# The next sequence's attention entry moved beside the experts, on one PSUM bank

## The reference, cut to what matters

```python
x = x + L0_attn(_layernorm(x))   # one head, softmax over queries, only the diagonal is used
x = x + L0_ffn(_layernorm(x))    # 2 layers: token shift, 8 heads of 64 with local windows of 64,
                                 # l2-normed rotary q and k, then norm, w1, gelu gate (341), w2
x = x + L1_attn(_layernorm(x))   # causal attention, 16 heads of 8, then Wo
x = x + L1_ffn(_layernorm(x))    # softmax router, top 2 of 8 experts, plus a shared expert:
    # y += gate[e] * (silu(x @ w_gate[e]) * (x @ w_up[e])) @ w_down[e]
```

## Time and profile before

| | us |
|---|---|
| median of three runs | 1863.35 (1860.35 to 1864.81) |
| profiled execution, its own time | 1865.29 |
| its span, first to last instruction | 1863.5 |
| busy PE / DVE / ACT / POOL | 1598.5 / 1239.7 / 926.7 / 594.0 |
| mean granted TensorE clock | 0.937 of full speed |

### The profile page before, as it was taken

How to read it: one execution, slowest core, us unless ns; L and a number is a source line. 1 busy time by engine, 2 the same in 40 slices (tenths; PEclk the granted TensorE clock), 3 DMA queues, 4 the chain that set the end, 5 groups by cost and what they waited for, 6 DMA issues and landing times.

```text
span 1863.5 us, 29596 instructions
## 1 busy us (share of the span) xinstructions
PE 1598.5 (86%) x11565; PEld 934.8 (50%) x11632; DVE 1239.7 (67%) x2636; ACT 926.7 (50%) x1751; POOL 594.0 (32%) x401
## 2 busy tenths in 40 slices
PE   5688876799979899799988999798996889788978
PEld 2354443446454555546555455545553546445635
DVE  6866767775677657595577756786576447674724
ACT  3465653466543844457544664438443444352241
POOL 2756726151160604324061511606043014110000
PEclk9789998799989999899998999899997899898989
DMA  4200100300131011500123001310114002304102
GB/s 120 66 1 21 27 1 20 69 23 17 41 89 32 22 32 34 111 23 2 41 68 69 22 24 34 92 29 22 32 40 105 3 18 76 78 11 103 37 1 63
DMA packets 37291, 80.12 MB, mean 43 GB/s; under 512 B 6782, under 2 KB 22654, under 8 KB 33776
## 3 DMA queue, kind: packets, MB, share of 16 engines
q1 hardware_dynamic: 37152, 78.22, 16.7%
HBM read 54.74 MB, written 8.78 MB: 34 GB/s over the span
## 4 chain that ended last, share of the span: by engine, by line
PE 47%; DVE 23%; ACT 14%; POOL 12%; issue 4%; DMA 0%; SPq 0%; POOLq 0%; DVEq 0%; ACTq 0%
PE ps L455 42%; POOL fsmall L1348 5%; DVE bsmall L1224 5%; ACT bigs L944 5%; PE ps L460 4%; POOL work L1371 3%; ACT work L870 3%; DVE fsmall L1113 2%; POOL work L1382 2%; POOL bsmall L1348 1%; DVE fsmall L1105 1%; DVE bxn L1021 1%; DVE work L1076 1%; DVE work L1075 1%; DVE fxn L1021 1%
## 5 line engine op out<-in xcount | busy, mean ns | idle before, releaser
L1348 POOL TENSOR_TENSOR fsmall<-fsmall,consts 128x8 f32<-128x8 f32 (+1 forms) x140 | 200.1, 1440 | 330.5 <-DVE fsmall L1015 310.9
L455 PE MATMUL ps<-maskb,identb 128*128 128x128 bf16 (+1 forms) x1122 | 227.8, 239 | 31.3 <-ACT work L870 18.8
L455 PE MATMUL ps<-bxt,mw 128*128 128x512 f32 x504 | 246.7, 610 | 5.9 <-DVE bigs L1320 5.9
L1371 POOL TENSOR_TENSOR work<-work 128x1024 f32<-128x1024 f32 x56 | 132.2, 2360 | 351.0 <-DVE work L1076 351.0
L870 ACT ACTIVATE work<-ps,fsmall 128x128 f32<-128x128 f32 x448 | 164.0, 493 | 71.1 <-DVE fsmall L1117 70.4
L460 PE MATMUL ps<-ident,work 128*128 128x128 f32 x924 | 140.6, 298 | 50.2 <-ACT work L870 42.4
L1224 DVE TENSOR_REDUCE bsmall<-ps 128x1 f32<-128x512 f32 (+3 forms) x308 | 175.3, 631 | 7.5 <-PE ps L455 6.8
L455 PE MATMUL ps<-wqkv,h 128*128 128x512 f32 x336 | 163.4, 618 | 14.1 <-ACT vs L830 8.8
L1402 POOL TENSOR_TENSOR work<-work,fsmall 128x1024 f32<-128x1024 f32 x56 | 106.2, 1897 | 216.1 <-DVE fsmall L1108 216.1
L944 ACT ACTIVATE bigs<-ps 128x512 f32<-128x512 f32 x280 | 146.1, 635 | 24.1 <-PE ps L455 23.7
L966 ACT ACTIVATE bigs<-ps 128x512 f32<-128x512 f32 x126 | 75.3, 598 | 156.6 <-PE ps L455 155.9
(11 more groups left out here) (327 smaller groups left out, 2962.7 us busy)
## 6 DMA issues: line engine op xcount, KB each, us to landing
mw<-in_experts SPq DMA_DIRECT2D x63, 384.0 KB, 3.1
pks<-scr_partsb SPq DMA_DIRECT2D x42, 192.0 KB
pqs<-scr_partsb SPq DMA_DIRECT2D x126, 64.0 KB
v2s<-vs SPq DMA_DIRECT2D x14, 512.0 KB, 4.7
v2s<-vs SPq DMA_DIRECT2D x14, 384.0 KB, 6.3
scr_partsb<-bigs SPq DMA_DIRECT2D x7, 768.0 KB, 3.7
wqkv<-in_experts SPq DMA_DIRECT2D x9, 384.0 KB, 3.1
xin<-in_x SPq DMA_DIRECT2D x7, 256.0 KB, 3.5
```

Of the source, the lines that this page charges most:

```text
L455: return nc.tensor.matmul(o, a, b, start=start, stop=stop, skip_group_check=True)
L1348: return nc.gpsimd.tensor_tensor(out, x, consts[:, k:k + 1].broadcast_to([x.shape[0], x.shape[1]]), op)
L1371: nc.gpsimd.tensor_tensor(R.qk[:, m, :], R.qk[:, m, :], R.part[m % 2], ALU.add).then_inc(R.l_add.sem, 1)
```

## The change

Lane B's entry for back s+1 is a generator of its own, `enter`, and is drawn beside the experts of back s: `beside` lets an entry stage go once the expert named in `ENTRY_AFTER` has passed. Back 0's entry stands behind `front0`; back 7's entry stays where it was. The entry uses bank 2 alone for the transposes, q, k and v, one after the other, so k waits for q's copy, v for k's copy. While it does, gate and up share two banks (`expert_banks`): a gate waits for the silu of the half expert before, an up for the multiply of the half expert before. In backs 6 and 7 there are three banks as before; back 0's and back 7's entries still use four. The normalised x goes to `bxe` in `ctmp`, the silu results have three buffers instead of four, so that `big[0]` to `big[2]` are free for the parts.

```diff
+ENTRY_AFTER = {"ln": 0, "xn": 1, "tp": 2, "q": 3, "k": 4, "v": 5, "parts": 5, "parts1": 5, "parts2": 6, "parts3": 6, "va": 5,
+               "save": 7}
+ENTRY_BANKS = [2, 2, 2, 2]
+def beside(experts, entry):
+    waiting = next(entry, None)
+    for name in experts:
+        e = int(name[3]) if name.startswith("moe") else int(name[2]) + 1
+        while waiting and e > ENTRY_AFTER[waiting]:
+            yield "n." + waiting
+            waiting = next(entry, None)
+        yield name
+    while waiting:
+        yield "n." + waiting
+        waiting = next(entry, None)
...
-        self.qkf, self.qkr, self.oc = ctmp[:, 0:2, :], ctmp[:, 2:4, :], ctmp
+        self.qkf, self.qkr, self.bxe, self.oc = ctmp[:, 0:2, :], ctmp[:, 2:4, :], ctmp[:, 2, :], ctmp
-        self.silu = [[self.big[2 * i + c] for c in range(2)] for i in range(2)]
+        self.silu = [self.big[i] for i in (3, 8, 9)]
...
+        def follows(R, s):
+            return R is backs and s + 1 < R.count
+        def expert_banks(R, s):
+            return 2 if follows(R, s) else 3
+        def entry_banks(R, s):
+            return [R.bb[i] for i in (ENTRY_BANKS if R is backs and s else range(4))]
...
+            def enter(R, s):
+                bt, bq, bk, bv = entry_banks(R, s)
                 yield "tp"
                 pe.wait_ge(R.b_xn.sem, R.b_xn.at(s, 1))
-                turn_tiles(R.bb[0], lambda tt: R.bxn[:, tt, :]).then_inc(R.b_tp.sem, 1)
-                yield "qkv"
+                turn_tiles(bt, lambda tt: R.bxn[:, tt, :]).then_inc(R.b_tp.sem, 1)
+                yield "q"
                 pe.wait_ge(R.b_xt.sem, R.b_xt.at(s, 1))
-                mm(R.bb[1], cw[:, 0, :], R.bxt[:, :]).then_inc(R.c_qkv.sem, 1)
-                mm(R.bb[2], cw[:, 1, :], R.bxt[:, :]).then_inc(R.c_qkv.sem, 1)
+                mm(bq, cw[:, 0, :], R.bxe).then_inc(R.c_qkv.sem, 1)
+                yield "k"
+                if bk is bq:
+                    pe.wait_ge(R.c_qkf.sem, R.c_qkf.at(s, 1))
+                mm(bk, cw[:, 1, :], R.bxe).then_inc(R.c_qkv.sem, 1)
+                yield "v"
+                if bv is bk:
+                    pe.wait_ge(R.c_qkf.sem, R.c_qkf.at(s, 2))
                 for tt in range(NT):
-                    i = mm(R.bb[3][:, tt * P:(tt + 1) * P], R.bxt[:, tt * P:(tt + 1) * P], cw[:, 2, :])
+                    i = mm(bv[:, tt * P:(tt + 1) * P], R.bxe[:, tt * P:(tt + 1) * P], cw[:, 2, :])
                 i.then_inc(R.c_qkv.sem, 1)
...
+                yield from beside(experts(R, s), enter(R, s + 1) if follows(R, s) else iter(()))
+            def experts(R, s):
+                banks = expert_banks(R, s)
...
-                            if n >= 3:
-                                q = n - 3
+                            if n >= banks:
+                                q = n - banks
                                 freed = R.m_hid if q % 2 else R.m_silu
                                 pe.wait_ge(freed.sem, freed.at(s, q // 2 + 1))
-                            mm(R.bb[n % 3], R.mw[:, e % SLOTS, j * MH + c * P:j * MH + (c + 1) * P], R.bxt[:, :]).then_inc(done.sem, 1)
+                            mm(R.bb[n % banks], R.mw[:, e % SLOTS, j * MH + c * P:j * MH + (c + 1) * P], R.bxt[:, :]).then_inc(done.sem, 1)
...
```

More of the change, by code:

```diff
@@ L56 @@
     "tensor": (
[L57 to L66, removed]
@@ L123, with ahead @@
 EXP_AT = exp_places()
+ENTRY_AFTER = {"ln": 0, "xn": 1, "tp": 2, "q": 3, "k": 4, "v": 5, "parts": 5, "parts1": 5, "parts2": 6, "parts3": 6, "va": 5,
+               "save": 7}
+ENTRY_BANKS = [2, 2, 2, 2]
+def ahead(entry):
+    return ("n." + name for name in entry)
+def beside(experts, entry):
[9 more added lines that the diff above has]
+        waiting = next(entry, None)
 def run_lanes(engine, order, front_lane, back_lane):
@@ L1174, in front, with enter @@
                 finish(R.fv)
-            def back(R, s):
+                if R is front0:
+                    yield from ahead(enter(backs, 0))
+            def enter(R, s):
                 R.bv.start()
@@ L1199, in back @@
                 tt_(R.parts[:, :, 2, :], R.qkr, R.parts[:, :, 1, :], ALU.subtract).then_inc(R.c_parts.sem, 1)
-                yield "va"
-                dve.wait_ge(R.c_qkv.sem, R.c_qkv.at(s, 3))
-                cp(R.va[:, :, :, 0:CD], R.bb[3][:, :].rearrange("p (a b c) -> p a b c", a=NT, c=CD)).then_inc(R.c_v.sem, 1)
+            def back(R, s):
+                x2q = x2[:, (R.first + s) % 3, :, :]
+                if R is back7:
+                    yield from enter(R, s)
                 def split_maxima(r, bank):
@@ L1297, in back, with experts @@
                 dve.wait_ge(R.r_w.sem, R.r_w.at(s, 1))
+                finish(R.bv)
+                yield from beside(experts(R, s), enter(R, s + 1) if follows(R, s) else iter(()))
+            def experts(R, s):
+                banks = expert_banks(R, s)
                 def add_expert(e):
@@ L1426, in back @@
                 finish(R.bp)
+                if follows(R, s):
+                    yield from ahead(enter(R, s + 1))
             run_lanes(pool, ORDER["gpsimd"], *both_lanes(front, back, fronts, front0, backs, back7))
@@ L1473, in front, with enter @@
                     yield from project(R, s, l)
-            def back(R, s):
-                last = s == R.count - 1
-                yield "parts"
+                if R is front0:
+                    yield from ahead(enter(backs, 0))
+            def enter(R, s):
+                yield "save"
                 sp.wait_ge(R.c_parts.sem, R.c_parts.at(s, 1))
@@ L1499, in back, with experts @@
                     sp.dma_start(R.pq[r][96:99, :, :], R.scrm.rearrange("k (a c) b -> k a (c b)", a=RH)).then_inc(R.c_mpacked.sem, 16)
+                yield from beside(experts(R, s), enter(R, s + 1) if follows(R, s) else iter(()))
+            def experts(R, s):
+                last = s == R.count - 1
                 for e in range(1, ALL):
```

93 lines of the change are left out of this document (58 added, 35 removed).

## The result

| kernel | median, us | runs | ratio to before |
|---|---|---|---|
| before | 1864.08 | 1860.35 to 1865.37 | |
| changed | 1835.59 | 1834.02 to 1835.88 | 0.9858 (0.9837 to 0.9879) |

The changed kernel is faster by 28.5 us, 1.4% (1.2 to 1.6%). The profiled execution took 1835.7 us with a span of 1833.9, against 1863.5 before.

A forecast was written before the change was run, and what follows sets the result against it. No engine reaches 90% (PE 86%); the chain of waits bounds the kernel, with the entry on it in the opening. Openings -32, first opening 0, experts' stretches +32.5, last part -30: -29.5, median 1834 us, range 1810 to 1860.

The forecast's parts named there:

- The opening: Front's local attention without the entry beside it: 8 us less per turn (5 to 9), -32 over four turns.
- The experts' stretch: Experts with the next entry beside them: 6.5 us more per turn, +32.5 over five turns (+5 to +60).
- The last part: After the turns, where backs set the pace: -19.5, +5 and -19.5 sum to -34, taken as -30 (-12 to -36).
- The signs: Profile: POOL roots 452 us over two turns; wrong if PE's waits for the multiply grow to tens of us.
- Rival 3: Last part gives only 12, as the seventh front or back 6's packed data come after the back: 1852, chance 0.14.
- Rival 5: Experts' stretch: two of four parts operations wait for a POOL sum of 2.36 us, +23.5: 1857, chance 0.05.
- the rule weighed in the prediction: A two-port DVE conversion or two-SBUF-input operation and a POOL instruction lock each other out for a whole instruction.
- two banks, 1.0 us: Early experts' stretch: an up waits for the previous half expert's multiply, 3 us late, two hidden: 1.0 per turn.
- rival 4: Two banks make PE wait for DVE, from moe61u to moe71u: 7.5 us more per turn, 1871, chance 0.14.
- The split of the +6.5: Experts' stretch: q and k 1.8, order 1.95, parts 0.3 and 1.9, moe61u -0.7, banks 1.0; sum 6.3, taken as 6.5.
- The first turn's opening: Back 0's entry pieces lie on DVE ahead of the front; it ends at 352 against 351.7: 0 (-5 to +5).
- rival 2: Experts' stretch hides nearly all of the entry, costing 2.5 us per turn: -51.5, 1812, chance 0.20.

The follow-up runs named there:

- e2: Changed kernel with back 0's entry put back in its old place in the first turn, all others ahead: 1832.45 us, ratio 0.9819 to the kernel before.
- e1: Kernel before with gate and up of backs 0 to 5 on two banks instead of three, entries and order as before: 1938.73 us, ratio 1.0411.
- e6: Kernel before with the changed kernel's order in the five turns, entries in old places, gate and up there on two banks: 1883.83 us, ratio 1.0110.
- e11: e1 with VectorE's dn1 and moe30u put ahead of the front's w1a0.1, w1a1.1, w1a2.1 in the five turns: 1921.60 us, ratio 1.0308.
- e8: Changed kernel with four front stages put ahead of an expert's stage on ScalarE, VectorE and TensorE in the five turns: 1850.08 us, ratio 0.9932.
- e5: Kernel before with the changed kernel's order in the five turns, entries in old places, three banks, last part as before: 1885.03 us, ratio 1.0117.
- e4: Kernel before with entries of backs 0 to 4 taken ahead, entries 5 and 6 in place, last part in old order: 1863.33 us, ratio 0.9994.
- e12: e2 with TensorE doing the front's last product w2.1 ahead of down product dn2 in the five turns: 1832.11 us, ratio 0.9823.
- e7: Changed kernel with third and fourth pieces of the parts split done a second time for backs 1 to 5: 1836.29 us, ratio 0.9861.

## Why the prediction was right

**Right, with its size.** *The opening*: -8 predicted, -7.1 in the windows, and the exponentials take 13.9 us where I had 12 to 13. *The turn*: 215 and 215.1. *The experts' stretch*: +6.5 and +6.0 (91 us as forecast, 90.5 measured). *The last part*: -30 and -31.9. *The signs*: POOL's roots come 451.5 us apart over the first two turns (303.73 to 755.22), where I had 452, and the idle time that ended with VectorE's product is 11.4 us (5.9 before), not tens. *Rival 3* had the front or the packed data late; the last transfers into the packed queries are issued by 759.5 in a turn, DMA is idle from 777 on (the last windows below), and the maxima start at 783. In the last part they start 9.7 us after `dn8` does, with the front's attention on the chain ahead of them and no idle time in front of them on TensorE, so the packed data don't hold them up. SP's rows:

```profile
745.56 0.43 SPq L1569 DMA_DIRECT2D scr_partsb<-bigs  x1
...
756.51 3.00 SPq L1580 DMA_DIRECT2D pqs<-scr_partsb  x9
```

*Rival 5*: of the seven first conversions of the parts none took longer than 689 ns, where one had 1355 (a row of the line over the whole run: min, median, max):

```profile
L1263 DVE CAST bigs<-ctmps x7: 686/689/689, 323.8 to 1545.3; 128x1024 bf16<-128x1024 f32 x7
```

In e2, where back 0's entry is in place, it is 1.37 us again. Both long ones began while POOL was at a product (the rows stand in the last section). In the changed kernel POOL is idle beside the parts, in the first turn (316.3 to 333.6) and beside this turn's experts (938.7 to 946.4, 950.4 to 954.4), so the rule weighed in the prediction was not put to the test there.

**The step that failed: two banks, 1.0 us.** I priced it from where VectorE is busy early in the stretch. Alone it costs 13.8 us in the stretch and 11.9 a turn (e1); rival 4 was to decide from 12.4 a turn for entry and banks together. In the new order it costs nothing (e6), and one difference between the orders is that VectorE's products stand ahead of the front's stages: moved forward in the old one they give some of it back (e11), moved back in the new one, with ScalarE's and TensorE's orders changed as well, they cost 4.5 in the stretch (e8). My argument against rival 4, "the multiplies are laid anew", held; it deserved a price of its own, and that is 5.5 us (e5), in the same stretch.

**The split of the +6.5.** I had given the order 1.95, q and k 1.8, the parts 2.2. Taken together, q, k, v and the parts are worth 0.8 (fifth turn of e4 against 91.8), the order 5.5. `dn2` ahead of `w2.1` is worth 0 (e12). `parts2` and `parts3` do hold up `rk1.0`, as these rows of VectorE and POOL say (idle 3.97 ahead of the sum, where the earlier trace rows had 0.67), and twice the work costs 1.8 more:

```profile
951.14 0.69 DVE L1269 CAST bigs<-ctmps 128x1024 bf16<-128x1024 f32 x1
951.86 1.23 DVE L1272 TENSOR_TENSOR bigs<-ctmps,bigs 128x1024 bf16<-128x1024 f32 x1
```

```profile
954.36 2.36 POOL L1452 TENSOR_TENSOR work<-work 128x1024 f32<-128x1024 f32 x1 [3.97 <-DVE work L1145]
```

but without them the stretch is only 0.8 shorter, so another path is almost as long there; which one, no run settled. The sum was right and its terms were not: that it came out at 6 is luck.

**The first turn's opening: 0, measured +5.8.** The products start 16.9 later, where I had 18. But VectorE takes up the front's first maximum only at 327.72, when clearings, `va`, the front's copy and the four parts are done [the chain above]; the products for it were ready some 6 us before, where I had counted 2.3. From the products to the end of `wo1` it is 38.0 us, where I had 31 (29 and 2.3); in the other turns it is 31.7. The bound was +5. e2 takes 3.8 of it back.

**The last part's terms.** The first block -19.5, measured -21.6 at back 5's router. Its experts +5, measured +13.0 (two more score stages of the front, `sm2.1` and `sm3.1`, now stand in them). The gap ahead of back 6's maxima -19.5, measured -25.4. They sum to -34.0, as predicted, and to -31.9 at the end; two errors of 8 and 6 have cancelled, which is luck too.

**What I had not seen** is that the turns give nothing. Five entries of seven, with all their openings and stretches, sum to +2.3 us. The prediction's own sum had it (-32 + 0 + 32.5), and rival 2, which hoped for a stretch longer by only 2.5, is refuted by the 6.0 of the changed kernel's turns and by e4.

## What to carry to other kernels

A buffer count is not priced by itself but together with the order of the engine that frees the buffers: one bank less cost 4% in one order and nothing in another, and the other order had a price of its own, 1.2%. Cross the parts of a change of schedule (old and new order, two and three banks, with and without the moved work) when you test it, since they need not add up. And where moved work is hidden in a pipelined turn, look whether the gain comes from the turn at all: here it came from the end, where the backs alone set the pace.

## What the runs showed of the hardware

What was lost ahead of the opening came back in it. In three kernels the experts' stretch changed while the turn did not: 91.8 and an opening of 29.4 (changed), 93.0 and 28.2 (e12), 93.6 and 28.0 (e7). Windows from 6.6, 9.2, 15.2 and 21.2 us after `sm0.0` on, of the changed kernel and then of e12 (the column behind the engines is the granted clock; a value between 0.50 and 1.00 is a window that has both levels in it):

```profile
762.50:765.10 2.60, 2.48 (x30) 1.68 (x34) 1.42 (x2) 2.60 (x8) 1.06 (x1) 0.50 0.96 180
765.10:771.10 6.00, 2.98 (x53) 1.89 (x46) 5.17 (x7) 3.58 (x11) 2.73 (x2) 0.96 0.64 155
771.10:777.10 6.00, 3.73 (x42) 3.24 (x40) 3.32 (x6) 3.44 (x9) 3.79 (x2) 0.61 0.23 81
777.10:780.10 3.00, 3.00 (x42) 2.55 (x42) 0.69 (x1) 1.17 (x2) 0.00 (x0) 0.64 0.00 0
```

```profile
759.10:761.70 2.60, 2.02 (x34) 1.23 (x34) 1.76 (x3) 2.60 (x8) 1.09 (x1) 0.73 0.99 217
761.70:767.70 6.00, 4.79 (x42) 3.29 (x42) 4.88 (x7) 4.16 (x13) 2.71 (x2) 0.50 0.53 183
767.70:773.70 6.00, 4.25 (x43) 3.71 (x43) 2.74 (x5) 3.06 (x9) 3.79 (x2) 0.50 0.04 11
773.70:776.70 3.00, 3.00 (x48) 2.63 (x46) 0.98 (x2) 1.56 (x3) 0.00 (x0) 0.96 0.03 5
```

In the changed kernel the clock is low (0.50, 1.2 GHz) under the third score product `sm2.0` (the first row), high (0.96, near 2.4 GHz) in the next window, in which TensorE is idle half of the time, and down to 0.61 and 0.64 when the long piece of transposes and products comes. In e12 it comes down only in the middle of `sm2.0` (0.73), stays at 0.50 in the next two windows and is back at 0.96 for the second part of the piece. Of the 1.2 us that e12's opening gives back, some 0.6 lie in the piece (from `pt1.0` to the end of `wo1.0` it takes 13.7 us, in the changed kernel 14.3) and some 0.6 ahead of it, where `sm2.0` takes 2.0 us and not 2.9. In e7 they are 0.9 and 0.5. So half a clock costs by what falls under it. That the clock is the cause of the even trade fits these rows; no run held the clock, so it is argued and not shown.

A conversion of the parts takes 0.69 us. The two long ones, in the kernel before and in e2, began while POOL was at a product of 1.90 us, and ended 0.5 to 0.6 us after it. Before (e2 has POOL's product at 326.83 and the conversion at 327.92):

```profile
324.83 1.90 POOL L1402 TENSOR_TENSOR work<-work,fsmall 128x1024 f32<-128x1024 f32 x1 [12.41 <-DVE fsmall L1108]
325.92 1.35 DVE L1190 CAST bigs<-ctmps 128x1024 bf16<-128x1024 f32 x1 [1.17 <-ACT ctmps L934]
```
